# A small memset behind every gather on GpSimd in an embedding-and-interaction kernel

## What is computed

```python
e = jnp.stack([tbl_0[ids[:, 0]], tbl_1[ids[:, 1]], ..., tbl_31[ids[:, 31]]], axis=1)   # (2048, 32, 64)
p, q = e[:, row_idx, :], e[:, col_idx, :]          # all pairs i < j
z = jnp.einsum('bpe,fpe,bpf->bp', p, kernel, q)    # kernel: (64, 496, 64)
h = jnp.concatenate([z, dense_ctx], axis=1)
h = jnp.maximum(h @ W_top1 + b_top1, 0.0)          # 512 -> 512
h = jnp.maximum(h @ W_top2 + b_top2, 0.0)          # 512 -> 256
y = h @ W_top3                                     # 256 -> 1
```

## Time and profile before

| | before |
|---|---|
| median of 3 runs | 1267.82 us (1261.34 to 1269.45) |
| span of the profiled execution | 1281.0 us |
| instructions | 16495 |
| mean clock of TensorE that was granted, as a share of full speed | 0.813 |
| busy share of the span: TensorE, VectorE, ScalarE, GpSimd | 66%, 51%, 53%, 38% |

### The profile page before, as it was taken

The page is one execution under the profiler, slowest core; times in us unless marked ns, Lnnn a source line. Parts: engine busy times, 40 slices in busy tenths (PEclk is TensorE's granted clock), DMA queues, the critical chain, the costliest instruction groups (busy, mean ns, idle before and its releaser), DMA issues.

```text
span 1281.0 us, 16495 instructions
## 1 busy us (share of the span) xinstructions
PE 845.6 (66%) x4672; PEld 330.6 (26%) x4672; DVE 656.8 (51%) x601; ACT 685.0 (53%) x5196; POOL 484.9 (38%) x518
## 2 busy tenths in 40 slices
PE   0570596603589658526899566028898856889999
PEld 0230253301344212102233122002233312223333
DVE  0350495401467445215689355016697545768881
ACT  0281295713255643106698525226696645779991
POOL 7557204575302454762400643755402244220000
PEclk9785697856789778757889777558899888889999
DMA  9111001111001110110101110210000101010000
GB/s 335 30 38 26 10 10 26 28 27 28 15 13 25 34 19 17 41 25 9 33 2 20 24 32 14 43 19 17 18 17 9 27 17 34 9 26 2 1 18 1
DMA packets 34644, 36.40 MB, mean 28 GB/s; under 512 B 18676, under 2 KB 20980, under 8 KB 34424
## 3 DMA queue, kind: packets, MB, share of 16 engines
q0 software_dynamic: 16384, 16.81, 7.1%
q1 hardware_dynamic: 18168, 18.53, 5.1%
HBM read 26.91 MB, written 0.01 MB: 21 GB/s over the span
## 4 chain that ended last, share of the span: by engine, by line
PE 45%; another core or an unknown queue 29%; issue 12%; DVE 11%; POOL 1%; DMA 1%; ACT 0%; DVEq 0%
PE y_ps L475 12%; PE y_ps L497 10%; PE sum_ps L511 8%; DVE batch_products L731 4%; DVE products L720 4%; PE layer_ps L527 4%; PE y_ps L490 3%; PE layer_ps L530 2%; DVE products L712 2%; PE y_ps L433 2%; POOL kept_rows L375 1%; PE y_ps L478 1%; PE y_ps L544 1%; PE y_ps L491 1%
## 5 line engine op out<-in xcount | busy, mean ns | idle before, releaser
L637 ACT ACTIVATE batch_products<-batch_products 128x64 f32<-128x64 f32 x2576 | 618.5, 243 | 298.8 <-issue 170.5
L375 POOL DMA_INDIRECT rows<-tbl_dram,idx x384 | 363.1, 945 | 613.3 <-PE y_ps L433 490.1
L637 ACT ACTIVATION_READ_ACCUMULATOR batch_products<-batch_products 128x1 f32 x2576 | 488.4, 190 | 123.2 <-issue 122.0
L720 DVE TENSOR_TENSOR products<-y_ps,xt 128x1024 f32<-128x1024 f32 (+1 forms) x224 | 258.5, 1200 | 260.8 <-remote 194.2
L475 PE MATMUL y_ps<-xt,kernel_sb 64*128 64x512 f32 (+1 forms) x448 | 233.3, 649 | 137.5 <-issue 78.5
L731 DVE TENSOR_TENSOR batch_products<-y_ps,kept_rows 128x1024 f32<-128x1024 f32 x192 | 225.5, 1217 | 92.7 <-remote 56.1
L497 PE MATMUL y_ps<-kernel_sb,xt 64*128 64x512 f32 x384 | 214.0, 683 | 71.7 <-DVE products L720 24.6
L476 PE MATMUL y_ps<-xt,kernel_sb 64*128 64x512 f32 (+1 forms) x448 | 233.4, 649 | 0.0
L499 PE MATMUL y_ps<-kernel_sb,xt 64*128 64x512 f32 x384 | 213.8, 683 | 0.0
L511 PE MATMUL sum_ps<-products,selector 128*32 128x512 f32 (+1 forms) x1520 | 162.4, 543 | 26.3 <-issue 10.9
L712 DVE TENSOR_TENSOR products<-y_ps,xt 128x1024 f32<-128x1024 f32 x68 | 79.8, 1218 | 160.5 <-remote 95.2
(11 more groups left out here) (54 smaller groups left out, 415.2 us busy)
## 6 DMA issues: line engine op xcount, KB each, us to landing
kernel_sb<-pair_kernel_dram SPq DMA_DIRECT2D x15, 512.0 KB, 4.9
rows<-tbl_dram,idx POOLq DMA_INDIRECT x384
special<-xt SPq DMA_DIRECT2D x48, 128.0 KB
kept_rows<-tbl_dram,idx POOLq DMA_INDIRECT x128
special<-xt SPq DMA_DIRECT2D x32, 64.0 KB
w_sb<-w_dram SPq DMA_DIRECT2D x1, 1024.0 KB
w_sb<-w_dram SPq DMA_DIRECT2D x1, 512.0 KB
kernel_sb<-pair_kernel_dram SPq DMA_DIRECT2D x1, 256.0 KB, 2.7
```

What stands on the lines that cost most here:

```text
L375: pool.indirect_dma_start(rows_of(g, q, t)[:, h, :], None, tables[j], bass.IndirectOffsetOnAxis(ap=idx[:, n, j:j + 1], axis=0)).then_inc(l ...
L637: last = nc.scalar.activation(product, product, ACT.Copy, accum_out=batch_sums(unit)[:, column:column + 1])
L720: nc.vector.tensor_tensor(into[:, :, 0:size], y[:, :, 0:size], by, ALU.mult).then_inc(unit_done, 1)
```

## The change

A buffer `pause` of 200 floats per partition is added. After every gather GpSimd writes zeros into it with one memset. Since all these memsets write the same buffer, each waits on the semaphore `paused` for the one before it. Nobody reads the buffer, and no other engine waits for `paused`.

```diff
+PAUSE = 200
...
+        pause = sb("pause", [P, PAUSE])
...
+        paused = sem("paused")
...
+            pauses = 0
             for g in range(len(SEGMENTS)):
...
                             pool.indirect_dma_start(rows_of(g, q, t)[:, h, :], None, tables[j],
                                                     bass.IndirectOffsetOnAxis(ap=idx[:, n, j:j + 1], axis=0)
                                                     ).then_inc(landed(g, q), 16)
+                            if pauses:
+                                pool.wait_ge(paused, pauses)
+                            nc.gpsimd.memset(pause[:], 0.0).then_inc(paused, 1)
+                            pauses += 1
```

## The result

The changed kernel takes 1183.75 us (median of 4 runs, 1179.83 to 1194.31), the kernel before 1267.3 us (median of 4 in the same session). The ratio is 0.936, 95% interval 0.931 to 0.941: 6.4% faster, where 30% was forecast. The profiled execution took 1181.42 us with a span of 1179.6 us, 101.4 us less than the 1281.0 us of before.

The account below looks back on a forecast made before the run. It took a backlog of gathers, 1.40 us each but issued every 1.25, to lock out the other engines. With the memset, 3 + 676 + 5 + 184 + 31 = 899 us, scaled to 890 us (-30%); range 850 to 1280 us.

Parts of the forecast that it names:

- the backlog never forms: GpSimd's gathers: at 1.51 us each they start slower than the 1.40 us each occupies, so other engines are not locked out.
- So I take 1.25 + 0.26 = 1.51 us: Pace of gathers on GpSimd: the memset's 0.26 us adds whole to 1.25 us, the idle 0.30 us staying with the gather.
- the threshold: Each gather keeps some shared thing occupied for 1.40 us; only a faster pace builds the backlog that locks out other engines.
- Both ends of the bound (1.25, 1.81): Pace of gathers in us: memset hidden completely in the idle time, or added with an idle 0.30 us on either side.
- rival 3: Half relief: other engines pass only in the 0.11 us free between two gathers; 1080 us, chance 0.10.
- the chain's nameless 41%: Share of the chain of waits that is nobody's work: 29% "another core or an unknown queue", 12% "issue"; read as lock-out.
- The sign: Whole kernel: faster by over 1%, chance 0.70 (relief and rival 3 together).
- As summed: Relief case: 448 gathers at the pace plus 3, 5, 184 and 31 us; 899 us at 1.51, chance 0.60.
- Without any lock-out the same work would take 847 us: Whole kernel: 1281 us less 499 us of locked-out stretches, plus 65 us of VectorE work done in them.
- What would show it: Signs listed beforehand in the new profile: gather pace, VectorE holes, ScalarE's step, chain shares, TensorE's clock, GpSimd's and TensorE's waits.
- Rival 1: Hidden and without effect: pace stays below 1.40 us, or 1.40 grows with the pace; backlog as before; 1268 us, chance 0.14.
- Rival 2: Slower: other engines stay cut off until GpSimd has worked off a run of gathers, memsets included; 1320 us, chance 0.16.

Follow-up runs that it names:

- pause1: The changed kernel with a memset of one float per partition instead of 200: 794.5 us (1.000) on one free core; 1284.9 us on an afflicted die's first core.
- fours: The changed kernel with no memset behind three of four gathers, three of 400 bf16 behind the fourth: 920.7 us (1.159) on one free core; 938.3 us afflicted first core.
- pause100: The changed kernel with 100 floats per partition in the buffer instead of 200: 818.3 us, 1.030 of the kernel before, on one free core.

## Why the prediction went wrong

**Where the 101 us come from.** The same two kernels on one core without the lock-out (another chip) split the gain. The lock-out costs the kernel before 1281.0 - 793.1 = 488 us and the changed one 1179.6 - 849.1 = 330.5 us: relief 157 us. The slower pace costs 849.1 - 793.1 = 56 us. The difference is the 101.4 us measured. It must be, since all four spans are measured and the free ones cancel; what the split shows is how large either part is.

**The step that failed** is "This is above 1.40 us, and by the reading above the backlog never forms". It failed twice, in the pace and in the threshold.

The first half is the memset's place. "So I take 1.25 + 0.26 = 1.51 us" rested on "the idle 0.30 us is the same to 0.01 us in every row, as if it belonged to the gather". The memset's own time was nearly right (0.28 us), but its start shows that only 0.17 us of the idle time stay and that 0.13 us of it can be filled. Both ends of the bound (1.25, 1.81) held; the middle that I picked was 0.115 us too high, and at 1.395 us the pace lies on the other side of 1.40. The Trainium skill's Perfetto Trace Analysis, "DMA Instruction — SWDGE (GPSIMD)", says that the processor still works on such a DMA behind the end that the profile shows. The trace doesn't contradict that, but the sum that I based on it, with the memset queued behind a tail of the full 0.30 us, gives 1.51 us where 1.395 were measured, and the measurement decides.

The second half is the threshold. With the pace at 1.48 us the first and third core of an afflicted die took 1117.4 and 1069.9 us (1020.7 to 1180.9 over four executions), not 890. The 1.40 us per gather describes the standstill at a pace of 1.25 us (core 4 with pause1 has the same holes, 39.0 and 10.2 us), but room above it doesn't end the lock-out. What was measured is a relief that grows with the time left over. Lock-out left on the afflicted die's first and third cores, each span less that of the same kernel alone on a free die (792.8, 849.1, 881.3, 920.0): 492 and 479 us at 1.25, 373 and 332 at 1.395, 236 and 189 at 1.48, 18 and 9 for fours. On the second and fourth core, against the same four spans, 547 and 538, 412 and 388, 330 and 318, 188 and 93 us are left. Taken as room per gather, the mean pace less ScalarE's step of 1.40 or 1.46 us in the kernel before, all of them fall into one order:

| room per gather, us | -0.25 | -0.15 | -0.065 | -0.005 | 0.02 | 0.08 | 0.08 (fours) | 0.17 (fours) |
|---|---|---|---|---|---|---|---|---|
| lock-out left, us | 547, 538 | 492, 479 | 412, 388 | 373, 332 | 330, 318 | 236, 189 | 188, 93 | 18, 9 |

Nothing special happens at zero. That is close to rival 3, "the others pass only in these gaps", to which I gave 0.10 and 1080 us. Why should others need more than a little room? That their own instructions use the same shared thing, so that the room must carry them, fits the order, and it fits that in the changed kernel, where more of them pass, ScalarE's period is 1.42 to 1.43 us, longer than both the 1.40 of before and the pace of 1.395; but it was only argued. fours and a uniform pace of 1.57 us weren't compared on an afflicted die. At 0.08 us of room fours leaves less than the even spacing does, but on other cores, so whether room in one piece helps more stays open.

**What held.** That the chain's nameless 41% was for the most part one mechanism and not a wait for data: without the lock-out its larger part, "another core or an unknown queue", is gone and 8% of "issue" are left, while gathers go on. The sign, faster, on this core. "As summed", 223 + 448 x pace: on free dies 810 against 816.5 us (pause100), 848 against 849.1 (the change), 886 against 881.3, 922 against 918.4, 1137 against 1145.6 (two memsets, 2.04 us). The sum was right to 1% wherever GpSimd is the bound; it was put in a place where GpSimd isn't. "Without any lock-out the same work would take 847 us" was 54 us too much (793.1), so the lock-out costs 488 us and not 434. The sum priced the standstills alone and not what follows them. TensorE comes out of one at a lower granted clock (0.82 in the third of the earlier trace rows), and its 4672 matmuls are busy for 845.6 us at a mean clock of 0.813 against 741.3 us at 0.998 without the lock-out. How many of the 54 us that accounts for was not measured.

**What would show it, point by point.** Gathers 1.45 to 1.6 us apart: no, 1.40. No hole of 10 us: no, 10.9 and 17.4. ScalarE at 0.12 us: no. "Issue" and "unknown" a few per cent of the chain: no, 30%. The clock mostly at the upper level: 0.60 in the long run, 0.848 on average against 0.813 before. GpSimd's wait under 100 us: no, 324.6. TensorE waiting for gathered rows instead: no, 28.3 us for the field pairs 0 to 3, where it was 26.2. "Partly filled" holes were named as the mark of rival 3, and partly filled they are.

**The rivals.** Rival 1 had the pace's side right (below 1.40) and the effect wrong: at 1.395 us, where a strict backlog forms every time, the lock-out shrank by 157 us. Rival 2 is excluded on the afflicted die, but its sign is right on a free one: there the change costs 7.0%, since GpSimd becomes the bound (45% of the chain in that run) and nothing is gained for it.

The Trainium skill (Runtime: NRT & Kernel Launch, "Instruction fetch mechanics") calls the cost of fetching instructions mostly hidden. The free die agrees: in 52 us TensorE's stream brings 453 matmuls beside 42 gathers. On the afflicted one it brings 22 in 51.4 us; no view shows the fetch itself, so whether it is the fetch that is held up there isn't shown. By that rule the change was to be worth nothing, as in rival 1; it was worth 6.4%.

**Open.** What is shared, why one die of a chip has the lock-out and the other not, and why ScalarE's step is 1.46 us on the second and fourth core of it and 1.40 on the first and third. That difference fits their being slower by 40 to 170 us, but no run shows that it is the cause.

## What to carry to other kernels

When several engines stop at once for "issue" and "remote", time the same program on a core of the other die before the kernel is changed: here that showed 789 to 829 us against 1270 to 1344, and a remedy that wins 6.4% on one die loses 7.0% on the other. Don't price an instruction that goes into the idle time behind a gather as added whole or hidden whole: look at how much of that time stays, here 0.17 of 0.30 us, and take both answers through to the end when a threshold lies between them. Where the lock-out has to be lived with, room given in one piece behind four gathers brought the span of one core from 1285 to 938 us and of its neighbour from 1339 to 1108, at 16% on a die that doesn't need it; no version here beats both kernels everywhere.

## What the hardware showed that I had not expected

- The same program takes 789 to 829 us on one die and 1270 to 1344 us on the other die of one chip, at the same time. It doesn't need neighbours: one core alone takes 1282 us. A second chip shows the same with a memset of one column added and the dies the other way round, 789 to 829 and 1272 to 1339 us.
- On the second and fourth core of each die, the free and the afflicted one, gathers start 1.21 us apart (0.27 us idle), on the first and third 1.25 (0.30 idle). In the lock-out ScalarE's step is 1.46 us on the former and 1.40 on the latter.
- A memset behind an indirect DMA starts the instant the DMA's bar ends and eats into the idle time: the bars of two gathers are 0.31 us apart with 0.12 us of memset between them, 0.45 with 0.28.
- A memset of 0.12 us behind every one of 512 gathers costs nothing where there is no lock-out (1.000, 0.999 to 1.001).
- On a free die neighbouring cores go in pairs: for the same kernel cores 6 and 7 above sit at a granted clock of 0.928 and 829 us, cores 4 and 5 at 1.000 and 789 to 793 us. Other executions have pairs between the two, 0.963 and 807 to 815 us.
